# GpSimd instead of VectorE for two rounding passes of the first FFN product's rows, from the second group of tokens on

## What is computed

```python
def _act_fake_quant(x, clip_factor):
    scale = jax.nn.sigmoid(clip_factor) * jnp.max(jnp.abs(x)) / QMAX      # one scale for all tokens
    return jnp.clip(_ste_round(x / scale), -QMAX - 1.0, QMAX) * scale     # QMAX = 127
...
x = x + _L0_xattn_ref(_layernorm(x), ctx_768, Wq, Wk, Wv, Wo, bo)
xq = _act_fake_quant(_layernorm(x), clip_x[0])
gate = jnp.einsum('bsh,ih->bsi', xq, _weight_fake_quant(w_gate))          # 512 -> 1408
up = jnp.einsum('bsh,ih->bsi', xq, _weight_fake_quant(w_up))
h = _act_fake_quant(jax.nn.silu(gate) * up, clip_down[0])
x = x + jnp.einsum('bsi,hi->bsh', h, _weight_fake_quant(w_down))          # 1408 -> 512
```

## Time and profile before

| | before |
|---|---|
| median of 3 runs | 547.33 us (546.87 to 547.88) |
| the profiled execution's own time | 547.3 us |
| its span in the trace | 545.5 us |
| mean granted PE clock | 0.999 |
| PE busy | 528.1 us (97%) |
| DVE busy | 475.3 us (87%) |
| ACT busy | 294.2 us (54%) |
| POOL busy | 231.8 us (42%) |
| first FFN product, from its first 128x512 matmul to the start of the last chunk | 311.69 to 459.39 us |

### The profile page before, as it was taken

How to read it: one execution, slowest core, us unless ns; L and a number is a source line. 1 busy time by engine, 2 the same in 40 slices (tenths; PEclk the granted TensorE clock), 3 DMA queues, 4 the chain that set the end, 5 groups by cost and what they waited for, 6 DMA issues and landing times.

```text
span 545.5 us, 8102 instructions
## 1 busy us (share of the span) xinstructions
PE 528.1 (97%) x2740; PEld 355.9 (65%) x2740; DVE 475.3 (87%) x879; ACT 294.2 (54%) x414; POOL 231.8 (42%) x349
## 2 busy tenths in 40 slices
PE   8989889999999999999999899999999999999997
PEld 7868678787888878888788644444444445544444
DVE  4966988999989899898989799999999988899884
ACT  4834645556465654554534646555545533999500
POOL 4385858769596895856553000000000000055442
PEclk9999999999999999999999999999999999999999
DMA  8809375765668465545949955850442220399987
GB/s 315 275 41 301 92 210 171 226 215 160 214 212 272 143 216 178 178 129 165 203 88 313 282 122 242 283 141 22 116 117 44 72 38 5 123 328 234 159 106 127
DMA packets 82943, 93.83 MB, mean 172 GB/s; under 512 B 47085, under 2 KB 50157, under 8 KB 82645
## 3 DMA queue, kind: packets, MB, share of 16 engines
q1 hardware_dynamic: 77877, 84.13, 49.9%
q0 software_dynamic: 4320, 7.87, 9.6%
q10 hardware_dynamic: 704, 1.31, 0.7%
HBM read 47.51 MB, written 37.78 MB: 156 GB/s over the span
## 4 chain that ended last, share of the span: by engine, by line
PE 73%; DVE 12%; SPq 6%; DMA 3%; issue 2%; ACT 1%; POOL 1%; ACTq 0%; DVEq 0%; POOLq 0%
PE SP L1137 13%; PE QO L1137 13%; PE QO L192 5%; PE QO L194 4%; PE QO L193 4%; SPq L37 4%; PE SP L463 4%; PE QO L1294 4%; PE PTP L1294 3%; PE SP L1294 3%; SPq L41 2%; PE MI L583 2%; PE MI L582 2%; PE MI L581 2%; PE WOP L1294 2%
## 5 line engine op out<-in xcount | busy, mean ns | idle before, releaser
L45 POOL DMA_DIRECT2D out<-n2b x30 | 30.3, 1045 | 207.4 <-DVE n2b L1327 207.4
L1144 ACT ACTIVATE sil<-QO,fsc 128x512 f32<-128x512 f32 x87 | 59.8, 687 | 70.9 <-PE QO L1137 69.3
L1137 PE MATMUL SP<-nT,wgu 128*128 128x512 bf16 x340 | 87.3, 379 | 0.4
L1137 PE MATMUL QO<-nT,wgu 128*128 128x512 bf16 x340 | 87.3, 379 | 0.1
L1148 DVE SCALAR_TENSOR_TENSOR h<-SP,fsc,sil 128x512 f32<-128x512 f32 x87 | 65.1, 748 | 8.7 <-PE SP L1137 7.1
L504 POOL TENSOR_TENSOR PN<-P,rs 128x512 f32<-128x512 f32 x64 | 44.3, 714 | 50.2 <-DVE rs L496 50.2
L1151 DVE TENSOR_REDUCE hmx<-h 128x1 f32<-128x512 f32 x87 | 59.7, 686 | 3.0
L487 ACT ACTIVATE P<-P,r 128x616 f32<-128x616 f32 x32 | 26.0, 812 | 63.7 <-DVE P L483 63.7
L1137 PEld LDWEIGHTS SP<-nT,wgu 128*128 128x128 bf16 x340 | 32.9, 98 | 41.4 <-DVE h L1148 2.5
L1137 PEld LDWEIGHTS QO<-nT,wgu 128*128 128x128 bf16 x340 | 33.2, 98 | 40.2 <-ACT sil L1144 0.3
L192 PE MATMUL QO<-xTs,wqs 128*128 128x512 f32 x124 | 50.4, 407 | 2.3 <-DVE xTs L223 2.0
(11 more groups left out here) (224 smaller groups left out, 1203.3 us busy)
## 6 DMA issues: line engine op xcount, KB each, us to landing
xTr<-in_xT SPq DMA_DIRECT2D x8, 1024.0 KB, 7.9
xn<-in_x SPq DMA_DIRECT2D x32, 256.0 KB, 3.8
out<-x SPq DMA_DIRECT2D x32, 256.0 KB, 2.9
n_rows<-n SPq DMA_DIRECT2D x32, 256.0 KB, 2.7
n2b<-n_rows SPq DMA_DIRECT2D x32, 256.0 KB, 3.8
out<-n2b POOLq DMA_DIRECT2D x30, 256.0 KB, 6.5
h_spill<-h SPq DMA_DIRECT2D x2, 2816.0 KB, 9.3
h<-h_spill SPq DMA_DIRECT2D x6, 768.0 KB, 7.2
```

Source lines behind the costliest of these rows:

```text
L1137: m = e.matmul(ps, wv_[:, k, col:col + 128], nT[:, b % 2, :, k, :], start=(k == 0), stop=(k == 3))
L1144: t_sil[n] = add("act", lambda e: e.activation(sil[:, n % SR, :], gp, ACT.Silu, scale=fsc[:, ic:ic + 1]), [t_g[n], t_fs, t_h.get(n - SR)], ...
```

## The change

For the groups 1 to 7 `quant_top` and `quant_low` are put into POOL's list instead of DVE's, under signals of their own (`x_qp`, `x_qp2`). Everything that waited for the two steps waits for the new signals. `quant_y` stays on ACT, and the order within each other list is kept.

```diff
         def quant_top(b, tt):
             n = 4 * b + tt
-            t_q1[n] = add("dve", lambda e: e.tensor_scalar(qb[:, tt, :], n2b[:, b % 2, tt, :], -MAGIC,
-                                                           127.0, ALU.add, ALU.min),
-                          [t_xy[n], t_qt.get(n - 4), t_g1], "x_q")
+            engine, sig = ("dve", "x_q") if b == 0 else ("pool", "x_qp")
+            t_q1[n] = add(engine, lambda e: e.tensor_scalar(qb[:, tt, :], n2b[:, b % 2, tt, :], -MAGIC,
+                                                            127.0, ALU.add, ALU.min),
+                          [t_xy[n], t_qt.get(n - 4), t_g1], sig)
 
         def quant_low(b, tt):
             n = 4 * b + tt
-            t_qd[n] = add("dve", lambda e: e.tensor_scalar_max(qb[:, tt, :], qb[:, tt, :], -128.0),
-                          [t_q1[n]], "x_q2")
+            engine, sig = ("dve", "x_q2") if b == 0 else ("pool", "x_qp2")
+            t_qd[n] = add(engine, lambda e: e.tensor_scalar_max(qb[:, tt, :], qb[:, tt, :], -128.0),
+                          [t_q1[n]], sig)
```

## The result

The changed kernel takes 571.09 us in the median of 3 runs (569.93 to 571.62), against 547.33 us before. The ratio is 1.0429 with a 95% interval of 1.0400 to 1.0458. The forecast was 546.4 us, the range 545.7 to 547.9 us. The sign, the size and the range were wrong; "slower" had 12 in 100.

A forecast was written before the change was run, and what follows sets the result against it. PE was taken to set the pace except in group 0, where it waits for DVE. Three stalls gone (-0.89 us), POOL's cost 0 and nothing else (0) turned 547.3 us into 546.4 us; range 545.7 to 547.9 us.

The forecast's parts named there:

- What bounds the kernel before: First FFN product: PE sets the pace in groups 1 to 6, so work taken from DVE there is worth 0.
- the three stalls: Group 0, chunks 2 to 7: PE's up products wait for DVE's h; all three waits go, -0.89 us.
- POOL's price: quant_top and quant_low on POOL, groups 1 to 7: 0.62 us for each pass, 1.24 us a tile.
- The late transfer: Rival, chance 0.10: POOL's passes delay the transposing transfer before the next group's first gate product; 547.8 or 551.9 us.
- the formula: Boundaries from groups 1 to 2 up to 6 to 7: each loses x - 0.43 us, 0.43 us being spare time.
- x: The us by which POOL's two passes for a tile together exceed 1.24 us; slower from x = 0.58 us on.
- The boundary from group 0 to 1, for which I saw room: Transfer into group 1: landing at 325.7 us before, due at 327.3 us, so no loss expected.
- Blocking: Rival, chance 0.03: POOL's passes hold up DVE, up to 558 us; expected 0, as h and hmx do not contend.
- SP, POOL's queue behind, the end of the product: SP's order stays, POOL has nothing behind the pairs until after 466 us, and all after the product only shifts: 0.

The follow-up runs named there:

- Run 5: Changed kernel with POOL's first pass as add and mult by 1, its second as min and max, same result: 546.14 us, ratio 0.9977 to the kernel before.
- run 7: Changed kernel, but POOL does only tiles 0 and 1 of groups 1 to 7, DVE tiles 2 and 3: 546.69 us, ratio 0.9987 to the kernel before.
- run 1: Changed kernel with POOL's minimum and maximum replaced by multiplications by 1, both bounds left out in groups 1 to 7: 550.4 us, ratio 1.0045.
- run 9: Changed kernel with 128x128 filler matmuls on PE before each group's first gate product, 15 ahead of group 1, 8 ahead of the others: 564.27 us, ratio 1.0316.
- run 2: Kernel before plus 22 POOL instructions (11 forms, twice) on tiles of their own in the first FFN product: 550.85 us, ratio 1.0047.
- run 3: Changed kernel with only quant_top on POOL in groups 1 to 7, quant_low back on DVE: 552.19 us, ratio 1.0073 to the kernel before.
- run 4: Changed kernel with only quant_low on POOL in groups 1 to 7, quant_top back on DVE: 553.23 us, ratio 1.0097 to the kernel before.
- run 10: Changed kernel with the next group's four tiles placed after chunks 0, 1, 2, 3 in every group: 564.89 us, ratio 1.0341 to the kernel before.
- run 8: Kernel before plus ten more forms of POOL's tensor_scalar, twice each, on tiles of their own: 550.12 us in a single execution.
- run 6: Changed kernel with filler matmuls on PE before each group's first gate product, 28 ahead of group 1, 14 ahead of the others: 570.82 us, ratio 1.0428.

## Why the prediction was wrong

**What bounds the kernel before: right.** PE sets the pace in all groups but the first, and the three stalls there were worth 0.9 us. They are gone in the changed kernel too, where the 12 sets of the chunks 2 to 7 took 10.37 us (311.35 to 321.72 us). Run 5 and run 7 gave a product of 146.8 us, against 147.7 us, and the forecast's -0.16% lies in both intervals (0.9965 to 0.9989 and 0.9975 to 0.9999).

**The step that failed is POOL's price.** "`quant_top` is that but for the second operation, so I take 0.62 us": the second operation was everything. `quant_top` took 1.93 us, `quant_low` 1.49 us, a tile with its waits 3.6 us instead of 1.4. As the upper bound I had 1.29 us, POOL's instruction with two inputs, so I took a pass that reads one tile to be no dearer; it was. The text named the doubt, that a minimum or maximum on POOL is on no row, but the range followed it only to 547.9 us, the case in which one pass costs 1.29 us.

**The late transfer: the right rival, with too small a chance.** Its mechanism, its place and its formula held: run 1 lost 0.44 to 0.49 us at four of the five boundaries measured where the formula gives 0.44, and 0.90 us at the one with the slower transfer. For the changed kernel, x = 3.42 - 1.24 = 2.18 us and 6 x 1.75 = 10.5 us; with -0.9 us the rival would have said 557 us. Two terms were missing in it. First, four tiles at 3.6 us are 14.3 us in a row: from 2.6 us after a group's start and with 4.3 us of transfer they make 21.2 us against 19.0, so that POOL's throughput and not its last tile set the length of a group, 2.2 us over at each boundary. The boundary from group 0 to 1, for which I saw room, was for the same reason the latest of all, 3.67 us: POOL's first pass started at 312.07 us, only 14.8 us before the gate product was due at 326.89 us, and its passes and the transfer took 18.6 us. Second, the clock.

**The clock was not in the prediction.** No stretch of the product before shows a lower clock. The granted clock fell to 0.90 to 0.93 in every second group. It fell behind the waits of 3.67, 2.05, 2.00 and 1.99 us, and stayed at 1.00 behind those of 1.91, 1.89 and 2.48 us. Where it had fallen, matmuls ran at half speed, 1.2 of 2.4 GHz, which cost 1.7 us each time, and filling the gaps took that away (run 9).

**Blocking: right that it costs nothing, for these instructions.** `h` had a median of 751 ns, against 750 ns before. But run 2 shows that the question was well put: DVE passes of the other kind rose to over 1 us beside POOL's work. How much it costs hangs on where they meet. The runs 3, 4 and 7 left a part of these passes on DVE, and there the longest was 295, 571 and 572 ns.

**SP, POOL's queue behind, the end of the product: right.** The part behind the product is 86.1 us in both.

## What to carry to other kernels

Price an instruction for GpSimd by a row with the same two operations in the same order; on 128x512, three forms that look alike cost 0.62, 1.49 and 1.93 us here. When the form is slow, look for another split of the same arithmetic: the same bounds in the order min and max, beside an add and mult, turned 4.3% slower into 0.2% faster. When work moves to an idle engine, check two things against the deadline of whoever waits: the last piece's delay, and the sum of all pieces of a period against the period less the fixed delays behind them (here 14.3 us against 19.0 - 2.6 - 4.3 = 12.1). If one of them fails, PE idles, and it can lose clock on top: here it did behind some gaps of about 2 us and more, and behind none of those up to 1.3 us in the runs 1, 3 and 4.

## What the runs showed of the hardware

- A GpSimd tensor_scalar of one operation takes 1.49 to 1.54 us on 128x512, longer than min and max together at 0.61 us or add and mult at 0.62 us; a copy takes 0.61 us. The order counts: min and max 0.61 us, max and min 1.93 us.
- The prices hardly depend on the number format, f32 or bf16; only mult and add varied, 0.62 and 0.76 us from f32 and 0.67 and 0.88 us from bf16, and why stays open. Add and min at 128x256 took 1.07 us and at 128x512 1.93 us, so about 3.4 ns an element and 0.2 us fixed; min and max 0.47 and 0.61 us.
- The Trainium skill (GPSIMD Engine Reference, Engine selection) calls one-input work on GpSimd roughly line-rate. Here add and mult come near that, 0.62 us against VectorE's 0.42 us for the first pass. The change's two passes do not, 1.93 and 1.49 us against 0.42 and 0.29 us; the measurement decides.
- GpSimd and VectorE at once: VectorE's f32 to bf16 and bf16 to bf16 tensor_scalar passes rose from 418 and 294 ns to up to 1039 and 1006 ns, while its two-input pass from PSUM and SBUF and its reduction kept 747 and 686 ns. GpSimd's 1.93 us pass took up to 2.14 us in run 7.
- In the changed kernel a gap of about 2 us in PE's work, once a group, was followed by the lower clock in every second group, not in each. In run 10 the lower clock came behind gaps of 3.65, 2.04 and 2.47 us, and not behind another one of 2.04 us. So the length of the gap alone does not tell; what does stays open.
- The same transposing transfer took 4.3 us each time in the kernel before and in the runs 2, 5, 7 and 8, and 4.7 to 5.2 us once or twice in each of the changed kernel and the runs 1, 3, 4, 6, 9 and 10. Why stays open.
